# Four matmul passes change their place in TensorE's queue: the products of `v` in the second phase of a three-phase kernel

## The reference

```python
x_in = concat([mem broadcast (64 rows), x], axis=1)          # 320 rows for each of 32 batches
q, k, v = x_in @ wq.T, x_in @ wk.T, x_in @ wv.T              # 4 heads of 32
attn = softmax(mask(q @ k.T / sqrt(32)))                     # j <= i and j > i - 64
out_swa = (attn @ v) @ wo.T
loss = 0.5 * sum((mlp(x_in) - out_swa) ** 2)                 # mlp: silu(x w1.T + b1) @ w2.T + b2
upd = (1 - alpha) * params - theta * grad(loss)              # over all rows of all batches
out_mem = mlp(x_in, upd)
out = g1 * out_swa + g2 * out_mem                            # gates: sigmoids of products
```

## Time and profile before

| | |
|---|---|
| median of 3 runs | 1404.73 us (1399.63 to 1407.65) |
| the profiled execution | 1401.96 us, span of the trace 1400.2 us |
| TensorE matmuls busy | 1326.6 us, 95% |
| VectorE busy | 1138.7 us, 81% |
| ScalarE busy | 932.6 us, 67% |
| GpSimd busy | 489.4 us, 35% |
| granted clock of TensorE, mean | 0.988 |

### The profile page before, as it was taken

The page is one execution under the profiler, slowest core; times in us unless marked ns, Lnnn a source line. Parts: engine busy times, 40 slices in busy tenths (PEclk is TensorE's granted clock), DMA queues, the critical chain, the costliest instruction groups (busy, mean ns, idle before and its releaser), DMA issues.

```text
span 1400.2 us, 33297 instructions
## 1 busy us (share of the span) xinstructions
PE 1326.6 (95%) x10635; PEld 855.6 (61%) x10635; DVE 1138.7 (81%) x2909; ACT 932.6 (67%) x2570; POOL 489.4 (35%) x815
## 2 busy tenths in 40 slices
PE   7889999999999999887899999999999998999996
PEld 5445555555555555544566666666666665888885
DVE  5889999999999999875777788877887775787876
ACT  2278888888888888875566665666566663555563
POOL 4446666666666666432001000100001000223232
PEclk9899999999999999999999999999999999999998
DMA  3222222222233332200001010010001001223221
GB/s 79 74 74 79 78 82 77 71 77 78 80 86 98 101 83 78 75 23 16 27 24 35 24 48 24 28 31 24 24 24 35 20 16 33 78 84 88 82 85 31
DMA packets 101968, 79.66 MB, mean 57 GB/s; under 512 B 13781, under 2 KB 95125, under 8 KB 101797
## 3 DMA queue, kind: packets, MB, share of 16 engines
q1 hardware_dynamic: 100820, 76.99, 19.6%
q10 hardware_dynamic: 976, 0.54, 0.2%
HBM read 49.70 MB, written 27.79 MB: 55 GB/s over the span
## 4 chain that ended last, share of the span: by engine, by line
PE 49%; issue 1%; DVE 1%; ACT 1%; POOL 0%; POOLq 0%; DVEq 0%; ACTq 0%
PE b_g L1348 4%; PE b_psD L1300 4%; PE b_psZ L1377 4%; PE b_psZ L1311 4%; PE d_psO L1903 4%; PE b_g L1361 4%; PE d_psH L1895 4%; PE b_psR L1354 3%; PE b_psM L1410 2%; PE b_psR L1370 2%; PE b_psL L1339 2%; PE b_psD L1400 2%; PE b_psM L1422 1%; PE b_psM L1430 1%; PE d_psG L1921 1%
## 5 line engine op out<-in xcount | busy, mean ns | idle before, releaser
L774 DVE TENSOR_REDUCE a_MX<-a_psS 128x4 f32<-128x1024 f32 x256 | 312.5, 1221 | 29.5 <-PE a_psS L296 29.3
L578 ACT ACTIVATE a_PT<-a_psE 128x512 f32<-128x512 f32 x504 | 273.1, 598 | 45.4 <-PE a_psE L313 45.3
L1760 POOL TENSOR_TENSOR b_SWB<-b_b2col,b_SW 128x128 f32<-128x128 f32 x65 | 25.9, 399 | 329.5 <-ACT b_SW L1494 329.5
L327 PE MATMUL a_psV<-a_PT,a_VX 128*32 128x256 f32 x2048 | 137.1, 385 | 0.2 <-ACT a_PT L578 0.2
L296 PE MATMUL a_psS<-a_KS,a_QS 48*128 48x256 f16 x1024 | 101.5, 276 | 17.3 <-DVE a_MX L774 14.0
L313 PE MATMUL a_psE<-a_QS,a_KS 50*128 50x256 bf16 x1008 | 97.7, 270 | 5.6 <-ACT a_PT L578 4.2
L1530 ACT ACTIVATE b_PR<-b_psL,b_mx 128x128 f32<-128x128 f32 x260 | 92.3, 365 | 3.0 <-DVE b_mx L1652 2.8
L1524 ACT ACTIVATE b_HT<-b_psR 128x512 f32<-128x512 f32 x65 | 38.8, 597 | 73.8 <-PE b_psR L1354 73.8
L327 PEld LDWEIGHTS a_psV<-a_PT,a_VX 128*32 128x32 f32 x2048 | 53.4, 109 | 51.1 <-issue 28.5
L296 PEld LDWEIGHTS a_psS<-a_KS,a_QS 48*128 48x128 bf16 x1024 | 30.1, 94 | 87.7 <-DVE a_MX L774 60.6
L1628 DVE SCALAR_TENSOR_TENSOR b_DZ<-b_U,b_psD 128x512 f32<-128x512 f32 x65 | 44.7, 688 | 43.7 <-PE b_psD L1300 42.8
(11 more groups left out here) (291 smaller groups left out, 3483.2 us busy)
## 6 DMA issues: line engine op xcount, KB each, us to landing
a_KS<-kparts SPq DMA_DIRECT2D x63, 192.0 KB
a_QS<-qparts SPq DMA_DIRECT2D x126, 96.0 KB
qparts<-a_QP SPq DMA_DIRECT2D x64, 96.0 KB, 2.2
a_X<-x_in SPq DMA_DIRECT2D x32, 128.0 KB, 2.2
kparts<-a_KP SPq DMA_DIRECT2D x64, 64.0 KB, 2.1
x<-a_X SPq DMA_DIRECT2D x32, 128.0 KB, 1.8
b_X<-x SPq DMA_DIRECT2D x32, 128.0 KB, 2.2
zT<-b_XT SPq DMA_DIRECT2D x32, 128.0 KB, 1.8
```

The lines of the kernel that those rows point to most:

```text
L327: mm = nc.tensor.matmul(psV[32 * h:32 * h + 32, 0:T], VX[:, b % UV, kt, at:at + 32], PT[:, gg, kt, h, :], start=(gg == 0 and kt == 0), sto ...
L578: nc.scalar.activation(PT[:, g % 2, :, h + s, :], shifted_bank(b, p, s), ACT.Exp).then_inc(S["exp"], 1)
L774: nc.vector.reduce_max(MX[:, b % 2, :].rearrange("q (s n) -> q s n", s=2)[:, :, 2 * p:2 * p + 2], psS[:], AX.X).then_inc(S["max"], 1)
```

## The change

In even slots, TensorE's step `v` of the next segment stands now ahead of `pt`, behind `dw2`; before, it was the slot's last step, behind `pv`. Nothing else is touched: the waits, the products and the banks are the same.

```diff
@@ -1451,6 +1451,8 @@
                 dw2(s - 1)
             if s % 2 == 1 and seg((s + 3) // 2):
                 zT((s + 3) // 2)
+            if s % 2 == 0 and seg((s + 2) // 2):
+                v((s + 2) // 2)
             if tile(s + 1):
                 pt(s + 1)
             if tile(s):
@@ -1459,8 +1461,6 @@
                 pv(s + 1)
             if s % 2 == 1 and seg((s + 3) // 2):
                 qk((s + 3) // 2)
-            if s % 2 == 0 and seg((s + 2) // 2):
-                v((s + 2) // 2)
```

## The result

The changed kernel takes 1412.93 us (median of 6 runs, 1410.91 to 1414.6); the kernel before, in 6 runs, 1403.98 (1399.63 to 1407.65). The ratio is 1.0061, with a 95% interval of 1.0046 to 1.0075: slower by 6.5 to 10.5 us. I had said 1413, and a chance of 0.76 for slower by more than 0.5%.

The account below looks back on a forecast made before the run. TensorE was taken to bound the second phase. 31 sets by 0.33 us give 10.2 us over the profiled 1401.96, so 1412.3 (1415.1 on the median); forecast 1413 us, range 1404 to 1420.

Parts of the forecast that it names:

- `v` starts 0.86 behind `dw2`, and the four passes take 0.45.: Front of the even tile: `v` starts at 710.42 with its inputs there; four passes at 0.11 each take 0.45 us.
- HT's wait hides 0.09; `pt` 0.36 later.: Between `dw2` and `pt`, even tile: the wait for ScalarE's copy HT hides 0.09 us of `v`; `pt` starts 0.36 later.
- `pt` to `pv` 1.42 in place of 1.45; `pv` 0.33 later.: Even tile: without a wait at `pt`, `pv` follows it by 1.42 us as in the odd tile, so 0.33 later.
- The removal at the back gains 0, and `dh` stays 0.92 behind `pv`, held by OT.: Even tile, `pv` to `dh`: OT's start, copy and reaction make 0.92 us without `v`; TensorE idles about 0.56, gain 0.
- `dw1` is not waiting; the odd tile moves as a block.: Odd tile: `dw1` starts 0.16 us behind DZ's end, behind other TensorE work, so earlier VectorE copies give nothing back.
- 31 sets by 0.33, 10.2 us.: Steady second phase: 31 sets of `v` products each cost 0.33 us, 10.2 us; the first set counts as 0.1.
- I say 1413.: Whole kernel: 1412.3 us from the profiled execution, 1415.1 from the median of runs; forecast time 1413.
- The rule of the Trainium skill, page "Perfetto Trace Analysis", section "Matmuls": Behind `pv`: `v` in bank psM covers OT's eviction of psD; by the rule the move opens a gap there.
- The 81 ns: Alternative price per 128-column matmul with weight loads: four would be 0.32 us, the shift 0.20, the sum 6.4 us.
- (a): Even tile, cost partly hidden, shift below 0.22 us: +0 to +7 us, 1402 to 1409; chance 0.18.
- (b): Front of the even tile: `v`'s first pass starts cold, OT answered in 0.19: +13 to +16 us, 1415 to 1420; chance 0.12.
- (c): Odd tile set by VectorE: earlier copies of V save up to 0.72 us a pair, 22 us, 1380; chance 0.06.

Follow-up runs that it names:

- run 4: Kernel before with all of `v` moved between `pred` and `pv` in even slots; ratio 1.0106 (1.0086 to 1.0126), pair 16.168 us.
- run 1: Kernel before with `v` cut to one single-column pass pair at its old place from segment 1 on; ratio 1.0016 (1.0006 to 1.0025), pair 15.722 us.
- run 5: Changed kernel with ScalarE's copy OT cut from 128 to 8 columns from the third tile on; one execution, 1412.86 us (before 1404.75).
- run 6: Kernel before with ScalarE's copy OT cut from 128 to 8 columns from the third tile on; one execution, 1402.14 us (before 1404.75).
- run 8: Kernel before with OT cut to 8 columns and one copy of V in place of three; one execution, 1399.71 us (before 1403.29).
- run 9: Kernel before with every product of `v` done twice at its old place behind `pv`; ratio 1.0092 (1.0068 to 1.0115), pair 16.167 us.
- run 7: Kernel before with one of VectorE's copies of V in place of three from the third segment on; ratio 1.0004 (0.9992 to 1.0016).
- run 2: Changed kernel with `v` cut to one single-column pass pair, ahead of `pt`; ratio against before 1.0026 (1.0015 to 1.0037), pair 15.788 us.
- run 3: Kernel before with one product of `v` moved ahead of `pt`, the other left behind `pv`; ratio 1.0022 (1.0009 to 1.0036).

## Why the prediction was right, step by step

- *`v` starts 0.86 behind `dw2`, and the four passes take 0.45.* Measured 0.86 and 0.44. The dearer rival, a slow first pass, did not come.
- *HT's wait hides 0.09; `pt` 0.36 later.* Measured 0.363 (medians of 6.620 against 6.257 us behind `qk`).
- *`pt` to `pv` 1.42 in place of 1.45; `pv` 0.33 later.* Measured 0.336. The 0.03 lies between `pt` and `pred`, 0.436 in place of 0.464, as `pt` no longer starts out of a wait; `pred` to `pv` stays 0.99. That PT sets `pv`, as I read ScalarE's rows, was wrong: run 4 shows the last 0.1 with PT long there. It did no harm, since PT and `pv` move together with `pt`.
- *The removal at the back gains 0, and `dh` stays 0.92 behind `pv`, held by OT.* Measured 0.919; run 1 shows the zero, run 5 that OT holds `dh`, run 6 that it did so before the change too, with ET ready 0.057 sooner. The trace of the kernel before had this in it, and I overlooked it. Behind the last segment there are no more `v` products, and its timeline has

```profile
1160.75 0.43 PE L1400 MATMUL b_psD<-b_PT,b_V 128*32 128x64 f32 x16
1161.67 1.10 PE L1300 MATMUL b_psD<-b_w,b_ET 128*128 128x512 f32 x2 [0.49 <-ACT b_OT L1553]
```

  the same 0.92 and the same 0.49 of idle time that the change made in every even tile.
- *`dw1` is not waiting; the odd tile moves as a block.* It does, at 16.060 - 15.726 = 0.334 for the pair and 0.335 at `dh`. But the slack of 0.16 that I gave `dw1` was mis-read (runs 6 and 8). It did no harm here, because with the products earlier DZ ends 0.30 ahead of `dw1` (717.14 and 717.44).
- *31 sets by 0.33, 10.2 us.* It was 30 by 0.334: at the set of 680.87 the slot has no `dw2`, `pt` waited 0.78 us for HT before and 0.33 after, and the products are free there as at the first set. With one long pair less, 9.7 us in the trace, 8.6 (6.5 to 10.5) in the timed runs.
- *"I say 1413."* That this meets the median of 1412.93 so closely is luck. 1413 lies between two sums, 1412.3 and 1415.1, on two readings of before that differ by 2.8, and the interval of the measured difference is 4 us wide. What was right by its mechanism is 0.334 a pair against 0.33.
- *The rule of the Trainium skill, page "Perfetto Trace Analysis", section "Matmuls"*, on the eviction of one group under the matmuls of the next, fits: the 0.49 us appear as soon as the group of the other bank is gone. The 81 ns of the Trainium skill, page "TensorE: Matmul & The Clock Gate", section "Back-to-back issue gap", does not fit these float32 passes: four take 0.44 us here, 0.11 each.
- *Rivals.* (a) would have needed a shift under 0.22. (b) needed a slow first pass; it took the 0.56 from `v` to `dh` for the price of four passes, but 0.45 are the passes, and in run 9 eight of them and the start of `dh` take 1.00. (c) is out by runs 1 and 7.

Open stays why the granted clock was lower in the kernels of runs 1 and 2, which were timed some 2 us above what their pairs give. No version here is faster than the kernel before with the whole computation; run 8 marks what a shorter OT and shorter copies of V together would be worth, 0.057 a pair; beyond that ET holds `dh`.

## What to carry to other kernels

A busy share of 99.9% did not say what was free and what was paid. Ask of each place in an in-order queue how long the wait is that stands there without filler, and whether the piece of work fits: inside it a piece is free, beyond it every pass is paid, so that moving work out of such a wait gains nothing and moving it to a place whose wait is covered already costs nearly all of it (0.33 of 0.45 us here). Look for a tile in the same trace where the piece is missing (the last one, often): it shows the wait bare. And where a cut gives nothing, two things may hold the place together, and only both cuts at once show it. Last, the start of a matmul's row can hide a wait: look at its weight load too.

## What the runs showed of the hardware

- `pv`, sixteen passes on 32-column weights, starts some 0.09 us later behind the passes of `v` and of `pred`, which have 128-column weights, than these follow each other, with PT long there (run 4: 0.54 us from `v` to `pv` for four passes of 0.11).
- The row of a matmul can start early or late against its weight load. `dh` starts 0.03 behind its load out of a wait and 0.11 behind it without one (before: 712.85 and 712.88; run 9: 746.68 and 746.79), and `z1` then follows `dh` by 0.93 or 0.86. From the load to `z1` it is 0.96 and 0.97.
- A weight load starts 0.11 us behind the end of ScalarE's OT (runs before, changed, 5) and 0.05 behind the end of VectorE's ET or DZ (runs 6, 9).
- Two passes that compute a single column but load 128 weights each hold the next group back by 0.14 us (run 2), where two of 128 columns take 0.22 (run 3): narrowing the moving side to 1 of 128 saves a third.
- ScalarE's copy out of a bank takes 0.18 us for 8 columns and 0.28 for 128.
